# A new order of the work in the attention of a six-block transformer kernel, and of one step in its recurrence

## The reference, cut to what matters

```python
x = x + 0.5 * _L0_ffn_ref(_layernorm(x), ...)    # F: 8 experts, all computed, weighted by a router
x = x + _L0_attn_ref(_layernorm(x), ...)         # R: chunked linear recurrence, 16 heads of 8
x = x + 0.5 * _L0_ffn_ref(_layernorm(x), ...)    # F
x = x + 0.5 * _L1_ffn_ref(_layernorm(x), ...)    # E: 8 small experts, the best one taken per token
x = x + _L1_attn_ref(_layernorm(x), ...)         # M: causal softmax attention, 16 heads of 8
x = x + 0.5 * _L1_ffn_ref(_layernorm(x), ...)    # E
```

```python
Q, K, V = qkv[0], qkv[1], qkv[2]
scores = jnp.einsum('bhsk,bhtk->bhst', Q, K) / sqrt(d_k)
probs = softmax(where(causal, scores, -inf), axis=-1)
attn = einsum('bhst,bhtk->bhsk', probs, V);  out = attn_cat @ w_o.T
```

## Time and profile before

| | before |
|---|---|
| median of 3 runs | 1594.37 us (1594.33 to 1596.65) |
| the profiled execution's own time | 1594.18 us |
| its span, first to last instruction | 1592.5 us |
| busy share of the span | PE 97%, DVE 79%, ACT 59%, POOL 59%, PEld 58% |
| mean granted TensorE clock | 0.994 of full speed |
| attention, middle batches | 31.4 us each, PE busy 31.23, DVE 30.6, ACT 27.7 |

### The profile page before, as it was taken

The page is one execution under the profiler, slowest core; times in us unless marked ns, Lnnn a source line. Parts: engine busy times, 40 slices in busy tenths (PEclk is TensorE's granted clock), DMA queues, the critical chain, the costliest instruction groups (busy, mean ns, idle before and its releaser), DMA issues. The chain is left out here.

```text
span 1592.5 us, 43234 instructions
## 1 busy us (share of the span) xinstructions
PE 1548.5 (97%) x15520; PEld 924.5 (58%) x15520; DVE 1260.7 (79%) x2662; ACT 936.0 (59%) x1826; POOL 935.5 (59%) x806
## 2 busy tenths in 40 slices
PE   7999999999999999899999999999999899999999
PEld 4666666666666666566666666666654334444444
DVE  7976776777877788786776777778778889999877
ACT  6755555555655334355555555556553378888842
POOL 2865756756754399875765756657456234444453
PEclk9999999999999999999999999999999899999999
DMA  4300000000001343100000000000001121112012
GB/s 162 106 8 5 7 0 7 7 0 7 8 1 34 55 82 66 42 9 1 8 1 6 7 0 7 7 0 8 5 11 34 41 57 41 35 42 62 9 42 60
DMA packets 74314, 43.33 MB, mean 27 GB/s; under 512 B 53818, under 2 KB 70842, under 8 KB 74052
## 3 DMA queue, kind: packets, MB, share of 16 engines
q1 hardware_dynamic: 74180, 41.56, 10.9%
HBM read 10.47 MB, written 2.10 MB: 8 GB/s over the span
## 5 line engine op out<-in xcount | busy, mean ns | idle before, releaser
L618 POOL TENSOR_TENSOR scratch<-scratch 128x512 f16<-128x512 f32 x379 | 441.6, 1166 | 375.7 <-ACT scratch L826 375.4
L1395 DVE SCALAR_TENSOR_TENSOR scratch<-psum,scratch 128x512 f32<-128x512 f32 x512 | 352.5, 689 | 235.5 <-PE psum L1979 213.1
L821 ACT ACTIVATE scratch<-psum 128x512 f32<-128x512 f32 x512 | 305.2, 597 | 394.7 <-PE psum L1979 393.8
L2021 PE MATMUL psum<-ffn_down_hi,scratch 128*128 128x128 f16 x2048 | 369.3, 219 | 0.3
L2023 PE MATMUL psum<-ffn_down_hi,scratch 128*128 128x128 f16 x2048 | 369.2, 219 | 0.0
L2022 PE MATMUL psum<-ffn_down_lo,scratch 128*128 128x128 f16 x2048 | 369.2, 219 | 0.0
L826 ACT ACTIVATE scratch<-scratch 128x512 f16<-128x512 f32 x512 | 318.6, 622 | 12.0 <-DVE scratch L1395 11.8
L2021 PEld LDWEIGHTS psum<-ffn_down_hi,scratch 128*128 128x128 f16 x2048 | 200.3, 98 | 59.1 <-POOL scratch L618 0.7
L2022 PEld LDWEIGHTS psum<-ffn_down_lo,scratch 128*128 128x128 f16 x2048 | 200.3, 98 | 58.0
L2023 PEld LDWEIGHTS psum<-ffn_down_hi,scratch 128*128 128x128 f16 x2048 | 200.4, 98 | 0.0
L1977 PE MATMUL psum<-x_hi,ffn_up_hi 128*128 (+1 forms) x512 | 194.1, 379 | 1.9 <-DVE scratch L1395 1.9
(11 more groups left out here) (223 smaller groups left out, 2711.0 us busy)
## 6 DMA issues: line engine op xcount, KB each, us to landing
scratch<-scratch SPq DMA_DIRECT2D x96, 128.0 KB, 2.7
raw<-in_ffn_w_dram SPq DMA_DIRECT2D x8, 768.0 KB, 4.3
ffn_up_hi<-scratch SPq DMA_DIRECT2D x32, 128.0 KB, 2.8
x_tok<-in_x_dram SPq DMA_DIRECT2D x8, 256.0 KB, 7.2
out_dram<-x_tok SPq DMA_DIRECT2D x7, 256.0 KB, 2.2
raw<-in_lin_dram SPq DMA_DIRECT2D x1, 1092.0 KB
x_hi<-scratch SPq DMA_TRANSPOSE x46, 2.3
x_lo<-scratch SPq DMA_TRANSPOSE x46, 2.3
```

The costliest lines, as they stand in the source:

```text
L618: pool.tensor_tensor(h_lo[r], h32[r], h_hi[r], ALU.subtract).then_inc(s_plo, 1)
L821: act.activation(gate_act[k % 2], bank(k % 2), ACT.Silu, scale=W_DOWN).then_inc(s_s, 1)
L1395: dve.scalar_tensor_tensor(h32[k % HSLOTS], bank(5 + k % 2), W_DOWN, gate_act[k % 2], ALU.mult, ALU.mult).then_inc(s_h, 1)
L2021: pe.matmul(dst, h_hi[r][:, cols], hi, start=k % FC == 0 and n == 0, stop=False, skip_group_check=True)
```

## The change

It moves instructions and gives banks out anew; no instruction of the four compute engines is added or dropped, nor any DMA, and nothing else is computed.

- Recurrence: for chunk 1 of the next batch, PE's `keys_values` goes ahead of `gn_rstd`, ACT's `values` ahead of `y_copy`, DVE's `weigh_keys` ahead of `normed`.
- Attention, every batch: the banks of the twelve tiles of a unit go round as 4, 7, 5, four times, in place of a sequence with 7, 4 and 5 mixed with the other users; the projections, the turned maxima and the tiles stand in a new order on PE and ACT; on DVE `prep_bn` goes one tile up, `spread` and `add` some tiles down.
- Attention, last batch: the norm for the next block's batch 1 is prepared earlier on DVE, POOL, ACT and SP, and the statistics of its batch 2 and the first `pick_expert` go into the batch.

The diff, cut to its core:

```diff
 # R: DVE (ACT: values(u + 5, 1) ahead of y_copy(b); PE: keys_values(u + 5, b + 1, 1) ahead of gn_rstd(b - 1))
+                    if more:
+                        weigh_keys(u + 5, 1)
                     if before:
                         normed(b - 1)
-                    if more:
-                        weigh_keys(u + 5, 1)
-                    if before:
                         gated(b - 1)
...
 # M: ACT, opening
-                exps(0, 0, 0, 7)
-                exps(0, 0, 1, 4)
+                exps(0, 0, 0, 4)
+                exps(0, 0, 1, 7)
                 exps(0, 0, 2, 5)
-                exps(0, 0, 3, 4)
+                exps(0, 0, 3, 7)
                 v_copy(0, 0, 7)
...
 # M: PE, opening
-                by_key(0, 0, 0, 3, 0, 4)
-                pe.wait_ge(s_p2exp, 3)
+                by_key(0, 0, 0, 3, 0, 7)
+                pe.wait_ge(s_p2exp, 6)
                 v_proj(0, 7)
                 by_query(1, 1, 5, 0)
...
 # M: DVE, body
                     if more:
-                        q_low(b + 1, 7)
-                        k_low(b + 1, 4)
+                        q_low(b + 1, 4)
+                        k_low(b + 1, 5)
                     maxima(u + 2, 2, 5)
+                    if not more:
+                        prep_bn(nx, SUB * bx)
                     maxima(u + 3, 3, 0)
...
+                    if not more:
+                        spread(nx)
...
+                    if more:
+                        prep_bn(nx, SUB * bx)
                     maxima(u + 3, 3, 5)
-                    prep_bn(nx, SUB * bx)
...
                     normalise(u, b, 0, odd)
-                    spread(nx)
+                    if more:
+                        maxima(u + 4, 0, 1)
...
                         maxima(u + 4, 0, 4)
+                        spread(nx)
+                        maxima(u + 4, 0, 5)
                     if before:
                         add(b - 1, 7)
...
                     normalise(u + 1, b, 1, odd)
+                    if not more:
+                        moe(nxt, (2, "spread"), False)
+                        moe(nxt, (2, "statistics"), False)
+                        moe(nxt, (0, 0), False)
...
                 moe(nxt, (0, 1), False)
-                moe(nxt, (2, "spread"), False)
-                moe(nxt, (2, "statistics"), False)
                 moe(nxt, (0, 2), False)
...
 # M: PE, body, the projections
                     if more:
                         pe.wait_ge(s_p2exp, KT * u + 8)
-                        q_proj(b + 1, 7)
-                        pe.wait_ge(s_p2exp, KT * u + 9)
-                        k_proj(b + 1, 4)
+                        q_proj(b + 1, 4)
                     by_query(u + 2, 2, 4, odd)
-                    pe.wait_ge(s_p2exp, KT * u + 10)
-                    by_key(u, b, 0, 8, odd, 5)
+                    pe.wait_ge(s_p2exp, KT * u + 9)
+                    by_key(u, b, 0, 8, odd, 7)
+                    if more:
+                        pe.wait_ge(s_p2exp, KT * u + 10)
+                        k_proj(b + 1, 5)
...
 # M: POOL, body
                     mask(u, 0, 3)
+                    if not more:
+                        prep_rstd(n0 + SUB * b + LEAD)
                     mask(u + 1, 1, 0)
+                    if not more:
+                        norm(b + 2)
                     mask(u + 1, 1, 1)
                     mask(u + 1, 1, 2)
-                    prep_rstd(n0 + SUB * b + LEAD)
+                    if not more:
+                        x_lower(n0 + SUB * b + LEAD)
                     mask(u + 1, 1, 3)
-                    norm(b + 2)
```

More of the change, by code:

```diff
@@ L764, in attention @@
                 for b in range(NB):
-                    u = NG * b
+                    u, more = NG * b, b < NB - 1
                     mask(u, 0, 0)
@@ L1247, in body @@
-                    exps(u + 2, 2, 9, 4)
+                    exps(u + 2, 2, 8, 4)
+                    exps(u + 2, 2, 9, 7)
                     exps(u + 2, 2, 10, 5)
-                    values(u + 1)
                     exps(u + 2, 2, 11, 4)
@@ L1252, in body @@
                         moe(nxt, (0, "exps"), False)
+                    values(u + 1)
                     exps(u + 3, 3, 0, 5)
-                    exps(u + 3, 3, 1, 7)
-                    exps(u + 3, 3, 2, 4)
+                    exps(u + 3, 3, 1, 4)
+                    exps(u + 3, 3, 2, 7)
+                    exps(u + 3, 3, 3, 5)
+                    exps(u + 3, 3, 4, 4)
+                    exps(u + 3, 3, 5, 7)
                     if more:
@@ L1792, in body @@
                         weigh(u + 4, 0)
-                    if before:
-                        normed(b - 1)
                     if more:
@@ L1797, in body @@
                     if before:
+                        normed(b - 1)
                         gated(b - 1)
@@ L1910, in body @@
                     if more:
-                        maxima(u + 4, 0, 1)
                         maxima(u + 4, 0, 2)
@@ L1919, in body @@
                     if more:
-                        maxima(u + 4, 0, 5)
                         maxima(u + 5, 1, 0)
                     normalise(u + 1, b, 1, odd)
+                    if not more:
+                        moe(nxt, (2, "spread"), False)
+                        moe(nxt, (2, "statistics"), False)
+                        moe(nxt, (0, 0), False)
                     if more:
@@ L1929, in body @@
                     normalise(u + 2, b, 2, odd)
-                    if not more:
-                        moe(nxt, (0, 0), False)
                 for b in range(NB):
@@ L2379, in body @@
                     outputs(u + 3, b, 3)
+                    if more:
+                        keys_values(u + 5, b + 1, 1)
                     if before:
                         gn_rstd(b - 1)
-                    if more:
-                        keys_values(u + 5, b + 1, 1)
                     if keys:
@@ L2555, in body @@
                         weighted_values(u - 1, b - 1, 3, 1 - odd, 0)
-                    by_key(u, b, 0, 6, odd, 4)
+                    if not before:
+                        pe.wait_ge(s_mv_in, b + 1)
+                    by_key(u, b, 0, 6, odd, 7)
                     by_key(u, b, 0, 7, odd, 5)
@@ L2614, in body @@
                         by_query(u + 4, 0, 0, 1 - odd)
+                    by_key(u + 2, b, 2, 0, odd, 7)
+                    by_key(u + 2, b, 2, 1, odd, 5)
+                    if more:
                         causal(0)
-                    by_key(u + 1, b, 1, 11, odd, 7)
+                    transpose_values(u)
+                    by_key(u + 2, b, 2, 2, odd, 4)
                     if more:
                         by_query(u + 4, 0, 1, 1 - odd)
-                    by_key(u + 2, b, 2, 0, odd, 4)
@@ L2677, in body @@
                         causal(0)
+                        by_query(u + 5, 1, 1, 1 - odd)
                     if before:
@@ L2680, in body @@
                     else:
-                        pe.wait_ge(s_p2exp, KT * (u + 2) + 11)
-                    by_key(u + 3, b, 3, 1, odd, 7)
-                    by_key(u + 3, b, 3, 2, odd, 4)
+                        pe.wait_ge(s_p2exp, KT * (u + 2) + 12)
+                    by_key(u + 3, b, 3, 2, odd, 7)
+                    by_key(u + 3, b, 3, 3, odd, 5)
+                    if not more:
+                        moe(nxt, (0, 0), False)
                     transpose_values(u + 1)
                     if more:
-                        pe.wait_ge(s_p2exp, KT * (u + 3) + 3)
+                        causal(1)
+                    by_key(u + 3, b, 3, 4, odd, 4)
+                    by_key(u + 3, b, 3, 5, odd, 7)
+                    if more:
+                        by_query(u + 5, 1, 2, 1 - odd)
+                        pe.wait_ge(s_p2exp, KT * (u + 3) + 6)
                         max_rows(u + 4, 0, 5)
@@ L2717, in body @@
                     weighted_values(u + 2, b, 2, odd, 3)
-                    by_key(u + 3, b, 3, 9, odd, 7)
-                    if not more:
-                        moe(nxt, (0, "bias 0"), False)
-                        moe(nxt, (0, 2), False)
                     if more:
                         by_query(u + 5, 1, 4, 1 - odd)
-                    by_key(u + 3, b, 3, 10, odd, 4)
+                    by_key(u + 3, b, 3, 9, odd, 4)
+                    if not more:
+                        moe(nxt, (0, 2), False)
+                    by_key(u + 3, b, 3, 10, odd, 7)
                     if more:
```

226 lines of the change are left out of this document (105 added, 121 removed).

## The result

The change makes the kernel slower: 1599.86 us, median of 9 runs (1598.75 to 1602.53), against 1595.01 us for the kernel before, median of 9 runs (1592.31 to 1596.65). The ratio is 1.0034, with a 95% interval of 1.0024 to 1.0044: +5.4 us, 3.8 to 7.0 (it goes by the means, 1594.8 and 1600.3; the medians lie 4.9 apart). I had said 1590.8 us, within 1586.5 to 1597.0, most likely faster.

What follows compares the result with a forecast made beforehand. It took PE and DVE as both full in middle batches, with most of the chain of waits through PE. Terms −0.5 + 0.7 − 2.45 − 1.3 = −3.55 us on 1594.18, plus 0.19 for the median, gave 1590.8 us, range 1586.5 to 1597.0.

Steps and rivals of the forecast that it cites:

- the last batch and the expert stage: Last attention batch and experts: earlier statistics shorten PE's x_lo wait by 0.7 us, fuller gaps give 0.6; −1.3 us.
- The clock: Batch 0: a clock dip goes (−2.2 us, 1588.5, chance 0.08) or one is added (1592.9, chance 0.04).
- The middle batches: Attention batches: filling three DVE waits for PE and two fewer work changes save 0.35 us a batch; −2.45 us.
- Rival (2): Middle batches: PE is the bound and the stalls only move; −1.15 us in all, 1593.0; chance 0.24.
- Rival (1): Middle batches: PE waits for ACT, 0.8 us a batch; +4.5 us in all, 1598.7; chance 0.19.
- the sign I had named for being wrong: Middle batches: `add` distance stays at 31.36 us or grows, with DVE waiting for the mask after `transpose_values`.
- Rival (4): Attention batches: DVE's joins move clear of POOL's selects (−2.7 us, chance 0.03) or another is hit (+2.7, 0.02).
- The opening: Attention's opening: `v_proj` waits for tile 3's exponential in bank 7, so DVE gets scores later; +0.7 us.
- The recurrence: Recurrence: two DVE waits in the last batch but one shrink or go, nothing gained in the others; −0.5 us.

Runs made afterwards that it cites:

- x8: x1 with tile 3 of unit 0 back in bank 4, so that `v_proj` does not wait for its exponential; 1594.24 us.
- x1: The changed kernel with only ACT's `x_upper` in the last attention batch moved later, behind the 2nd exponential of unit u + 2; 1598.05 us.
- x4: The kernel before with only the early preparation of expert batch 1 (statistics, normalisation, copies, transposes) in the last attention batch; 1598.88 us.
- x2: The changed kernel with 60 small matmuls on PE ahead of tile 9 of unit u + 1 in the last batch, ACT's wait kept; 1596.43 us.
- x7: The kernel before with PE's gaps in the attention's opening and first batch filled by 20 and 16 more small matmuls; 1589.58 us.
- x3: The kernel before with the change of the recurrence alone; 1595.64 us, ratio 1.0009.

## Why the prediction was wrong

At clock 0.992 the steps are: before 1595.5; the change without its two mistakes (x8) 1594.6; with the opening's wait (x1) 1595.9; with ACT's early copy 1598.0. The clock adds the rest: from 0.9927 to 0.9889 is 3.8 us. Together 2.5 + 3.8 = 6.3 us, the distance of the means, 1594.7 and 1601.0; for the first 9 runs of the change, at 0.9897, it is 2.5 + 3.0 = 5.5, the +5.4 of the result.

- **The step that failed** is the term "the last batch and the expert stage. −1.3 us, bounds 0 and −3.1". It priced what the move of expert batch 1's preparation does to DVE (1.4 us) and to SP (two issues), and not what it does to ACT: `x_upper` went past 26 exponentials to a place where its input, three steps away over DVE and POOL, had not been made. The rows to see it by were there: POOL's normalisation and ACT's exponentials can be placed in time from the middle batches. Measured: +2.1 us of stall (x1 against the change); x4, the move by itself, costs 2.7 ± 0.4, of which PE's own wait is 1.8. The bound "0" had no ground, since a reason that excluded a loss was never given. The rest of the term was half right: the wait for x_lo fell from 1.21 to 0.44 us, and as I had written, by 0.7; a new wait of 0.39 us and one of 0.88 where it had been 0.57, 0.7 us together, gave it back right behind, most likely by the DVE step that POOL now holds for 1.26 us.
- **The clock** was a rival with 0.04 for a dip more, and only for the opening, priced at 2.2 us. It is the larger half of the loss, 3.8 us, and x2 gives back all of it by filling one wait of 3.67 us. It does not hang on that wait alone: x1, which has no such wait, has a mean clock of 0.9907, about half of the way back to 0.9927. I had read the clock in one profiled execution and took its low stretches for the kernel's own; they differ from run to run.
- **The middle batches**, −2.45 us: DVE's waits ahead of `add` and of the last tile of unit `u + 3` went, as said, and the period fell by 0.03 us in place of 0.35; −0.2 in all. Rival (2), PE as the bound, was right, and the chain in the earlier trace rows had said so. The 0.1 us for a change of work, "from the starts", does not show. Rival (1) did not come as a cost: no wait of PE stands in the middle batches of the changed kernel at all. But DVE does wait for the mask, 0.38 us a batch at the start of each (1395.36), and the distance of 31.33 is nearly the old 31.36; that is close to the sign I had named for being wrong. One part of DVE's waits was filled and another took its place. Rival (4), the joins: the one that took 0.56 us takes 0.17 at 1394.31, another takes 0.41 at 1410.37, and the four of a batch 0.92 us together in place of 1.20. The period does not show this either, DVE not being the bound.
- **The opening**, +0.7 us with an upper bound of +1.0: right in sign and mechanism, measured 1.3 ± 0.4. DVE's wait did not grow as I said (2.18 us against 2.41), since in this execution the clock was at its upper level around tile 3, which took 0.38 us at 1263.49 and not 0.60.
- **The recurrence**, −0.5 us: −0.3 ± 0.3 at equal clock. In the last batch but one both waits went, as said; in the others 0.02 to 0.13 us a batch were lost, with `weigh_keys` waiting 0.31 us for ACT, where I had said that nothing would change.
- **The chances**: 0.43 for faster rested on two terms, −2.45 and −1.3, the first a gain from waits of an engine that was not the bound, the second without a price for what it moved on ACT.

## What to carry to other kernels

A chain of steps that is moved ahead must be checked link by link: when each input is made, and what stands queued behind the engine that waits for it; if that engine empties the buffers of the bounding one, the wait stalls both. Where a filled wait is not on the bounding engine, price it at nothing. And read the mean clock of every run beside its time: 7 us of 1594 came from 80 small matmuls in PE's gaps, more than from any reordering here.

## What the runs showed of the hardware

- The mean granted clock of one and the same program went from 0.988 to 0.997 from run to run, with a time from 1589.6 to 1600.6 us; 0.001 of it is 0.99 us. Three quarters of the variance of the kernel before is this.
- No hole of some microseconds is needed for a fall of the clock. In the kernel before PE was busy 2.05 of 3.50 us from 1251.5 on, in pieces with gaps of 0.41 to 0.58 us, and the clock behind it was 0.50. By the Trainium skill, page "TensorE: Matmul & The Clock Gate", section "A second HAM failure mode: psum-queue depth-cycling", a PE that idles briefly but often between groups of matmuls can bring its clock down as well; by that rule, the trace agrees, and x7 shows that filling the gaps takes the fall away.
- Even that is not all: x1's clock fell behind a stretch with 2.47 of 3.40 us busy, and x3's behind one with 2.92 of 3.41, while in the profiled execution of the kernel before, whose attention is that of x3, it stood at 1.00 through the last batch, in the same place with 3.06 of 3.41 and 7 us later even with 2.90 of 3.41. What decides in such a stretch was not tried and stays open, as does whether the opening's wait lowers the mean clock by itself (x1 0.9907, x8 0.9923, 12 runs each, and the runs of one kernel scatter by 0.002).
